# Last sums of a hybrid block: four parts in place of eight, shared by VectorE and GpSimd

## The chip, the cores and the metric

The kernel runs on one core of one Trainium2 chip. The metric is the device time in microseconds of one execution; a profiled execution also has a span, from its first to its last instruction. Engines are named as in the profile: PE is TensorE, DVE is VectorE, ACT is ScalarE, POOL is GpSimd, SP is SyncE, which here only issues DMAs. A q behind a name (SPq, ACTq) means the engine's sequencer, which issues DMAs and waits.

## The reference, cut to what matters

```python
x = x + conv_attention(group_norm(x))            # x: (32, 16, 16, 64) f32
t = to_tokens(x)                                 # 8192 tokens of 64 channels
t = t + axial_attention(layer_norm(t))
t = t + mixture_of_experts(layer_norm(t))        # 8 experts, each token goes to 2 of them
# inside: out = gate1 * expert1(token) + gate2 * expert2(token)
```

Only the last line concerns the change. For every token the result is the residual `t`, plus the gated output of its first expert, plus that of its second: two additions over 8192 x 64 numbers.

## The kernel before

The tokens lie as 128 partitions x 64 tiles x 64 channels: partition p holds tokens 64p to 64p + 63. The residual stays in SBUF the whole time (`s.x1`, called residual in the rows). The expert stage works through 39 slot tiles of tokens sorted by expert. GpSimd scatters each result row with an indirect DMA (line 1243) to `chosen_out` in HBM, which has one row of 64 floats for each token and each of its two choices. Every semaphore `added` counts the landed scatters.

After the last slot tile comes the final stage, with which the change deals:

- SP waits until all scatters have landed (`all_added`, line 1157). Then it issues eight loads of 512 KB (line 1194), two for each quarter of the tiles: the quarter of the first choices into `first`, that of the second choices into `second`. Both are halves of the buffer called norm_T in the rows. Semaphore `fin_in[q]` counts the two loads of quarter q (16 each).
- VectorE goes through eight parts of 8 tiles (`PARTS_OUT = 8`, so `EIGHTH = 8`). For each it waits for the quarter in which the part lies, adds `second` to `first` in place (line 1769), waits for that sum, and adds `first` to the residual (line 1771). The latter counts up `sum_n`.
- SP and ACT each wait for `sum_n` of a part, and each issue two stores of it (line 1160, called from two loops). A store takes 32 partitions of the part and writes rows of 256 bytes that lie 1 KB apart in the output.
- SP and ACT end when all stores have landed. GpSimd only waits in `all_added`, and does nothing else in this stage. TensorE and ACT's compute are done too.

```python
out_rows = out_dram.rearrange("b r c e -> b (r c) e").rearrange("b (g j) e -> j b g e", j=4)

def store(eng, q, j):
    eng.dma_start(out_rows[j][:, part(q), :], s.x1[j * BATCH:(j + 1) * BATCH, part(q), :]).then_inc(stored, 16)
```

The order of work on each engine is that of the code. Semaphores alone tie the engines together. SP's queue holds the eight loads and, behind them, SP's stores; ACT's queue holds only its stores.

Of the kernel before, what the change touches and what calls it, by code (L numbers as in the profile page):

```python
# [14 lines left out]
ALU = mybir.AluOpType  # L15
# [6 lines left out]
TOK = BATCH * L  # L22
# [659 lines left out]
QUARTERS = 4  # L682
# [306 lines left out]
EXPERTS, HID = 8, 682  # L989
# [5 lines left out]
REGION = TOK // SLOT  # L995
# [22 lines left out]
    return next(t for t in range(len(TABLES)) if k < sure_tiles(t) or t == len(TABLES) - 1)  # L1018

PARTS_OUT = 8

def dispatch_and_experts(nc, s, a, out_dram, sem):

    with ExitStack() as own:
# [22 lines left out]
        number, base, first_slot, tile_base = (tmp(f"rt_{n}", [P, EXPERTS]) for n in ("number", "base", "first_slot", "tile_base"))  # L1050
# [95 lines left out]
        EIGHTH = TILES // PARTS_OUT  # L1146
        first, second = (s.xt[:, i * TILES * C:(i + 1) * TILES * C].rearrange("p (t c) -> p t c", c=C) for i in range(2))
        fin_in = [sem(f"fin_loads{q}") for q in range(QUARTERS)]
        half_n, sum_n, stored = sem("fin_first_added"), sem("fin_both_added"), sem("fin_stored")
        out_rows = out_dram.rearrange("b r c e -> b (r c) e").rearrange("b (g j) e -> j b g e", j=4)  # L1150

        def part(q):
            return slice(q * EIGHTH, (q + 1) * EIGHTH)

        def all_added(eng):
            for i, landed in enumerate(added):
                eng.wait_ge(landed, adds(len(range(i, FTILES, len(added)))))
# [7 lines left out]
        with nc.Block() as block:  # L1165
            @block.sync
            def _(eng):
                eng.wait_ge(pads_n, 1)
                for i in range(2):
                    eng.dma_start(s.router[halves(i), i * EXPERTS:(i + 1) * EXPERTS], a["L1_ffn_router_w"].rearrange("e c -> c e"),  # L1170
                                  allow_slow_non_contiguous=True).then_inc(router_n, 16)
                landed = 0
                for k in range(FTILES):
                    t = table_of(k)
                    eng.wait_ge(tab_n, t + 1)
                    for m in range(landed, chunks_in_table(t)):
                        eng.wait_ge(sent[m], 16 * 2 * PAIR)
                    landed = chunks_in_table(t)
                    wait(eng, gate_n, k - 3)
                    wait(eng, ext_n, k - 3)  # L1180
                    tile = eng.value_load(table[t][0:1, k:k + 1], min_val=0, max_val=BLANK)
                    src = slot_x[bass.ds(tile, 1), 0:width(k), :]
                    for band in range(4):
                        lane = band % 2 * B32
                        eng.dma_start(x[k % 4][band * B32:(band + 1) * B32, 0:width(k)].rearrange("t (b c) -> t b c", c=B32),
                                      src[:, :, lane:lane + B32].rearrange("o (b t) c -> (o t) b c", t=B32)).then_inc(x_in[k % 4], 16)
                    eng.dma_start(gate_id[k % 4][0:depth(k), :, :], src[:, :, C:C + 2].rearrange("o (r p) c -> (o p) r c", p=depth(k)),
                                  allow_slow_non_contiguous=True).then_inc(x_in[k % 4], 16)
                eng.wait_ge(oc_n, FTILES)
                all_added(eng)  # L1190
                for q in range(QUARTERS):
                    some = slice(q * QTILES, (q + 1) * QTILES)
                    for k, into in enumerate((first, second)):
                        eng.dma_start(into[:, some, :], s.chosen_out[k * TOK:(k + 1) * TOK, :].rearrange("(p t) c -> p t c", p=P)[:, some, :]
                                      ).then_inc(fin_in[q], 16)
                for q in range(PARTS_OUT):
                    eng.wait_ge(sum_n, q + 1)
                    for j in (2, 3):
                        store(eng, q, j)
                eng.wait_ge(stored, 16 * PARTS_OUT * 4)  # L1200

            @block.gpsimd
            def _(eng):
                eng.memset(s.router[:, :], 0.0).then_inc(pads_n, 1)
                eng.memset(chosen[:, :, 0], 0.0).then_inc(const_n, 1)
                eng.memset(going_on[:, :, 0], 0.0).then_inc(const_n, 1)
                eng.memset(going_on[:, :, 1:PAIR + 1], 1.0).then_inc(const_n, 1)
                for i in range(2):
                    eng.memset(full[i][:, :], 0.0).then_inc(const_n, 1)
                    eng.memset(end[i][:, :], 0.0).then_inc(const_n, 1)  # L1210
                eng.memset(one_row[:, :], 1.0).then_inc(const_n, 1)
                eng.memset(table_f[:, :], float(BLANK)).then_inc(const_n, 1)
                eng.memset(ones[:, :], 1.0).then_inc(order_n, 1)
                for t, n, first, by in ((number, EXPERTS, EXPERTS, -1), (base, EXPERTS, 0, TOK), (first_slot, EXPERTS, 0, TOK), (tile_base, EXPERTS, 0, REGION),
                                        (step, REGION, SLOT, SLOT), (tile_no, FTILES, 0, 1)):
                    eng.iota(t[:, :], pattern=[[by, n]], base=first, channel_multiplier=0,
                             allow_small_or_imprecise_dtypes=True).then_inc(const_n, 1)
                eng.wait_ge(order_n, 1)
                eng.affine_select(out=lower[:, :], in_=ones[:, :], compare_op=ALU.is_gt, fill=0.0, base=0,
                                  pattern=[[1, P]], channel_multiplier=-1).then_inc(order_n, 1)  # L1220
                for k in range(2):
                    eng.iota(ids[:, k, :], pattern=[[1, TILES]], base=k * TOK, channel_multiplier=TILES,
                             allow_small_or_imprecise_dtypes=True).then_inc(ids_n, 1)

                def send(m, first, last, at_once):
                    if first == 0:
                        eng.wait_ge(slots_n, m + 1)
                        eng.wait_ge(rows_n, m + 1)
                        eng.wait_ge(z_n, Z * (m + 1))
                    for t in range(first, last):  # L1230
                        for k in range(2):
                            tile = m * PAIR + t
                            eng.indirect_dma_start(s.slot_x[:, :], bass.IndirectOffsetOnAxis(slot[:, k, tile:tile + 1], 0),  # L1233
                                                   rows[m % RING][:, k, t, :], None).then_inc(sent[m], 16)
                        if (t + 1 - first) % at_once == 0 or t == last - 1:
                            eng.wait_ge(sent[m], 16 * 2 * (t + 1))

                def scatter(k):
                    eng.wait_ge(oc_n, k + 1)
                    for j in range(R):  # L1240
                        if j > 0 and k + 2 < FTILES:
                            eng.wait_ge(h_n, HCHUNKS * (k + 2) + j + 1)
                        eng.indirect_dma_start(s.chosen_out[:, :], bass.IndirectOffsetOnAxis(ex_id[k % OUTS][0:depth(k), j:j + 1].bitcast(U32), 0),  # L1243
                                               out[k % OUTS][0:depth(k), j, :], None, bounds_check=2 * TOK - 1, oob_is_err=False).then_inc(added[k % OUTS], 16)

                eng.wait_ge(s.blank_n, 16)
                send(0, 0, PAIR, 1)
                send(1, 0, PAIR, 1)
                send(2, 0, 4, 1)
                send(2, 4, PAIR, 2)  # L1250
                send(3, 0, PAIR, 2)
                for k in range(FTILES):
                    m, piece = 4 + k // 3, k % 3
                    if m < PAIRS:
                        send(m, (0, 3, 6)[piece], (3, 6, PAIR)[piece], 3)
                    scatter(k)
                all_added(eng)

            @block.tensor
            def _(eng):  # L1260
# [138 lines left out]
            def _(eng):  # L1399
# [23 lines left out]
                for g in range(STEPS):  # L1423
# [9 lines left out]
                    m = chunk(g, 4)  # L1433
# [46 lines left out]
                copy_y(LAST)  # L1480
                for q in range(PARTS_OUT):
                    eng.wait_ge(sum_n, q + 1)
                    for j in (0, 1):
                        store(eng, q, j)
                eng.wait_ge(stored, 16 * PARTS_OUT * 4)
# [2 lines left out]
            def _(eng):  # L1488
# [276 lines left out]
                run(eng, body, tab_n)  # L1765
                result(LAST, LAST % OUTS)
                for q in range(PARTS_OUT):
                    eng.wait_ge(fin_in[q * QUARTERS // PARTS_OUT], 32)
                    eng.tensor_tensor(first[:, part(q), :], first[:, part(q), :], second[:, part(q), :], ALU.add).then_inc(half_n, 1)
                    eng.wait_ge(half_n, q + 1)  # L1770
                    eng.tensor_tensor(s.x1[:, part(q), :], s.x1[:, part(q), :], first[:, part(q), :], ALU.add).then_inc(sum_n, 1)  # L1771

def hybrid_block(nc, a, out):
# [59 lines left out]
```

## Time and profile before

| | us |
|---|---|
| time, median of 3 runs (lowest, highest) | 971.08 (970.32, 974.22) |
| span of the profiled execution | 969.5 |
| last scatter issued by GpSimd | 945.90 |
| first final load issued by SP | 947.96 |
| first final sum starts on VectorE | 953.26 |
| last final sum starts on VectorE | 963.32 |

The profiled execution has no device time of its own in the profile: its span is 969.5 us, 0.8 us under the fastest of the three timed runs and 1.6 us under their median. The lower four lines are starts inside that span. The final stage, from the first load to the end, is 21.5 us long, 2.2% of the span.

### The profile page before, as it was taken

How to read it: one execution, taken by the hardware profiler on the slowest of the kernel's cores; microseconds unless marked ns; L12 is line 12 of the kernel's file. 1: busy time of each engine (PE TensorE's matmuls, PEld its weight loads, DVE VectorE, ACT ScalarE, POOL GpSimd, SP SyncE). 2: the span in 40 equal slices, each digit the busy share in tenths (PEclk: the TensorE clock that was granted, in tenths of full speed). 3: DMA queues.
4: the chain of work that ended last, by engine and by line, in shares of the span. 5: the costliest groups of instructions: out<-in, count | busy, mean ns of one | idle time of the engine just before them, and what ended most of it. 6: DMA issues, size and time to landing. Idle time of an engine off the chain costs nothing.

```text
span 969.5 us, 24022 instructions
## 1 busy us (share of the span) xinstructions
PE 829.5 (86%) x8420; PEld 505.2 (52%) x8420; DVE 623.7 (64%) x1425; ACT 456.7 (47%) x894; POOL 411.0 (42%) x524
## 2 busy tenths in 40 slices
PE   4775699999999788979998877869989999999940
PEld 4544477777777665647777752223323333333430
DVE  0452487878787466753887956768756666667644
ACT  2042466666666434444554534634535555555520
POOL 0000255555545311100245555666676774444570
PEclk9975799999999879998998889989989999999985
DMA  7115300000000199000000041052133332232108
GB/s 195 55 54 123 65 9 11 8 11 8 11 8 5 54 341 328 6 2 3 11 18 19 20 65 31 24 78 44 36 57 54 57 58 46 43 48 34 20 3 260
DMA packets 156254, 56.29 MB, mean 58 GB/s; under 512 B 121103, under 2 KB 150617, under 8 KB 156176
## 3 DMA queue, kind: packets, MB, share of 16 engines
q1 hardware_dynamic: 142736, 45.69, 20.9%
q0 software_dynamic: 9088, 8.55, 2.7%
q10 hardware_dynamic: 4352, 1.05, 0.5%
q8 instruction: 45, 0.74, 0.3%
q14 instruction: 33, 0.27, 0.1%
HBM read 25.09 MB, written 28.51 MB: 55 GB/s over the span
## 4 chain that ended last, share of the span: by engine, by line
PE 35%; DVE 10%; issue 4%; POOL 3%; DMA 2%; ACT 1%; SPq 1%; ACTq 0%; DVEq 0%; POOLq 0%
PE bank L1352 17%; PE bank L1362 9%; PE bank L1292 2%; POOL chosen_out L1243 2%; PE bank L1370 2%; POOL slot_x L1233 1%; PE bank L1283 1%; DVE norm_T L1751 1%; PE bank L1265 1%; PE bank L1274 1%; PE bank L1301 1%; DVE av_og L1501 1%; DMA slot_x<-rows,slots 1%; ACT norm_T L1459 1%; DVE residual L1771 1%
## 5 line engine op out<-in xcount | busy, mean ns | idle before, releaser
L1352 PE MATMUL bank<-ex_xt,ex_w 64*114 64x512 f32 (+7 forms) x936 | 216.6, 587 | 27.0 <-DVE ex_xt L1696 13.2
L1751 DVE TENSOR_TENSOR norm_T<-norm_T,bank 114x512 f32<-114x512 f32 (+7 forms) x234 | 142.0, 630 | 100.4 <-ACT norm_T L1459 98.5
L1243 POOL DMA_INDIRECT chosen_out<-ex_out,ex_id x156 | 153.2, 982 | 118.0 <-DVE norm_T L1751 42.0
L1459 ACT ACTIVATE norm_T<-bank 114x512 f32<-114x512 f32 (+7 forms) x234 | 129.9, 558 | 93.4 <-PE bank L1352 92.2
L1233 POOL DMA_INDIRECT slot_x<-rows,slots x128 | 125.3, 979 | 111.3 <-issue 64.4
L1352 PEld LDWEIGHTS bank<-ex_xt,ex_w 64*114 64x114 f32 x936 | 76.6, 178 | 142.7 <-issue 105.2
L462 POOL TENSOR_TENSOR probs<-shifted,win_rden 128x512 f32<-128x512 f32 x64 | 66.8, 1044 | 103.3 <-DVE win_rden L656 96.7
L1362 PE MATMUL bank<-norm_T,ex_w 114*64 114x512 f32 (+7 forms) x468 | 101.9, 571 | 0.3 <-ACT ex_w L1446 0.3
L642 DVE TENSOR_REDUCE win_max<-ps_s 128x8 f32<-128x512 f32 x64 | 43.9, 686 | 35.8 <-PE ps_s L502 35.8
L1362 PEld LDWEIGHTS bank<-norm_T,ex_w 114*64 114x64 f32 x468 | 30.1, 138 | 67.9 <-issue 49.8
L1452 ACT ACTIVATE norm_T<-bank 128x512 f32<-128x512 f32 (+7 forms) x39 | 21.8, 559 | 79.9 <-PE bank L1362 79.9
L647 DVE TENSOR_TENSOR shifted<-ps_s,win_max 128x512 f32<-128x512 f32 x64 | 44.2, 691 | 4.7
L527 PE MATMUL ps_c<-xp,tap_w 128*128 128x256 f32 x288 | 45.6, 304 | 0.0
L596 ACT ACTIVATE shifted<-shifted 128x512 f32<-128x512 f32 x64 | 40.3, 631 | 10.9 <-DVE shifted L647 9.8
L652 DVE TENSOR_REDUCE win_den<-shifted 128x8 f32<-128x512 f32 x64 | 43.2, 675 | 0.1
L1292 PEld LDWEIGHTS bank<-wo_sb,av_og 128*128 128x128 f32 x256 | 31.9, 203 | 18.2 <-DVE av_og L1501 11.4
L587 ACT ACTIVATE values<-ps_yv 128x512 f32<-128x512 f32 x32 | 19.1, 598 | 44.5 <-PE ps_yv L510 44.5
L1292 PE MATMUL bank<-wo_sb,av_og 128*128 128x64 f32 x256 | 34.2, 290 | 6.5 <-DVE av_og L1501 6.5
L845 POOL TENSOR_TENSOR residual<-residual,bo_sb 128x512 f32<-128x512 f32 x8 | 10.2, 1269 | 69.6 <-DVE ax_xc L949 69.6
L938 DVE COPY ax_y<-ax_ps_y 128x512 f32<-128x512 f32 x32 | 22.1, 692 | 27.0 <-PE ax_ps_y L872 26.8
L630 DVE COPY score_side<-ps_yv 128x512 f32<-128x512 f32 x32 | 22.1, 690 | 26.3 <-PE ps_yv L489 26.3
L527 PEld LDWEIGHTS ps_c<-xp,tap_w 128*128 128x128 f32 x288 | 39.0, 191 | 0.0
(259 smaller groups left out, 1482.9 us busy)
## 6 DMA issues: line engine op xcount, KB each, us to landing
slot_x<-blank SPq DMA_DIRECT2D x1, 17028.0 KB, 56.3
ex_x<-slot_x SPq DMA_DIRECT2D x128, 64.0 KB
norm_T<-chosen_out SPq DMA_DIRECT2D x8, 512.0 KB, 7.0
w_in<-in_L_ffn_w_dram SPq DMA_DIRECT2D x24, 168.0 KB
chosen_out<-ex_out,ex_id POOLq DMA_INDIRECT x156, 2.2
wlocal_in<-in_L_conv_w_local_dram SPq DMA_DIRECT2D x2, 1152.0 KB, 7.4
norm_T<-in_x_dram SPq DMA_DIRECT2D x4, 512.0 KB, 8.8
residual<-in_x_dram SPq DMA_DIRECT2D x4, 512.0 KB, 7.6
```

The lines of the kernel that those rows point to most:

```text
L462: eng.tensor_tensor(probs[e][:, :, :], shifted[e][:, :, :], rden[e][:, :].unsqueeze(2).to_broadcast([P, HEADS, WTOK]), ALU.mult).then_inc( ...
L527: last = eng.matmul(ps_c[:, 0:L].rearrange("p (r c) -> p r c", r=SIDE), s.tap_w[:, tap].rearrange("p k c -> p (k c)"), xp[par][:, u:u + SI ...
L642: eng.tensor_reduce(mx[e][:, :], scores(e), AX.X, ALU.max).then_inc(max_n, 1)
L647: eng.tensor_tensor(shifted[e][:, :, :], scores(e), mx[e][:, :].unsqueeze(2).to_broadcast([P, HEADS, WTOK]), ALU.subtract).then_inc(sub_n, 1)
L652: eng.tensor_reduce(den[e][:, :], shifted[e][:, :, :], AX.X, ALU.add).then_inc(den_n, 1)
L1233: eng.indirect_dma_start(s.slot_x[:, :], bass.IndirectOffsetOnAxis(slot[:, k, tile:tile + 1], 0), rows[m % RING][:, k, t, :], None).then_i ...
L1243: eng.indirect_dma_start(s.chosen_out[:, :], bass.IndirectOffsetOnAxis(ex_id[k % OUTS][0:depth(k), j:j + 1].bitcast(U32), 0), out[k % OUTS ...
L1292: last = eng.matmul(ps_r[:, t * C:(t + 1) * C], og[g % 2][:, m, t * P:(t + 1) * P], s.wo[:, m, :], start=(m == 0), stop=(m == 1))
L1352: eng.matmul(ps[b][0:HCHUNK, 0:width(k)], w13[par][halves(i), c * HCHUNK:(c + 1) * HCHUNK], xt[par][halves(i), 0:width(k)], start=True, st ...
L1362: last = eng.matmul(ps_y[halves(i), 0:width(k)], w2[par][:, c, :], h[par][:, c, 0:width(k)], start=(pair == 0), stop=(pair == PAIRS_OF_CHU ...
L1459: eng.activation(act[c % DEEP][:, 0:width(k)], ps_1[c % DEEP][0:HCHUNK, 0:width(k)], ACT.Silu).then_inc(act_n, 1)
L1751: eng.tensor_tensor(h[par][:, c, 0:width(k)], act[c % DEEP][:, 0:width(k)], ps_3[c % deep3(k)][0:HCHUNK, 0:width(k)], ALU.mult).then_inc(h ...
```

## The change

`PARTS_OUT` goes from 8 to 4, so a part is a quarter of 16 tiles, and a store moves 128 KB in place of 64 KB; there are 16 stores in place of 32, with the same rows of 256 bytes. Of each part VectorE sums the first ten tiles and GpSimd the last six, each with the same two additions. GpSimd waits for `fin_in[q]` in place of `all_added`. SP and ACT wait for both engines' sums before they store a part. The renaming of loop variables on GpSimd (`first` to `start_at` and `begin`) only keeps the name `first` free for the buffer.

```diff
-PARTS_OUT = 8
+PARTS_OUT = 4
...
+        pool_half_n, pool_sum_n = sem("fin_first_added_pool"), sem("fin_both_added_pool")
...
+        def mine_and_pools(q):
+
+            cut = q * EIGHTH + 10
+            return slice(q * EIGHTH, cut), slice(cut, (q + 1) * EIGHTH)
...
                 for q in range(PARTS_OUT):
                     eng.wait_ge(sum_n, q + 1)
+                    eng.wait_ge(pool_sum_n, q + 1)
                     for j in (2, 3):
                         store(eng, q, j)
...
-                all_added(eng)
+                for q in range(PARTS_OUT):
+                    some = mine_and_pools(q)[1]
+                    eng.wait_ge(fin_in[q], 32)
+                    eng.tensor_tensor(first[:, some, :], first[:, some, :], second[:, some, :], ALU.add).then_inc(pool_half_n, 1)
+                    eng.wait_ge(pool_half_n, q + 1)
+                    eng.tensor_tensor(s.x1[:, some, :], s.x1[:, some, :], first[:, some, :], ALU.add).then_inc(pool_sum_n, 1)
...
                 for q in range(PARTS_OUT):
                     eng.wait_ge(sum_n, q + 1)
+                    eng.wait_ge(pool_sum_n, q + 1)
                     for j in (0, 1):
                         store(eng, q, j)
...
                 for q in range(PARTS_OUT):
-                    eng.wait_ge(fin_in[q * QUARTERS // PARTS_OUT], 32)
-                    eng.tensor_tensor(first[:, part(q), :], first[:, part(q), :], second[:, part(q), :], ALU.add).then_inc(half_n, 1)
+                    some = mine_and_pools(q)[0]
+                    eng.wait_ge(fin_in[q], 32)
+                    eng.tensor_tensor(first[:, some, :], first[:, some, :], second[:, some, :], ALU.add).then_inc(half_n, 1)
                     eng.wait_ge(half_n, q + 1)
-                    eng.tensor_tensor(s.x1[:, part(q), :], s.x1[:, part(q), :], first[:, part(q), :], ALU.add).then_inc(sum_n, 1)
+                    eng.tensor_tensor(s.x1[:, some, :], s.x1[:, some, :], first[:, some, :], ALU.add).then_inc(sum_n, 1)
```

GpSimd's last instructions before the change are the scatters and nothing behind them:

```order
L1243 DMA chosen_out<-ex_out,ex_id 16384x64 x112
L1165 UNCONDITIONAL_BRANCH
```

After the change eight additions stand behind the scatters:

```order
L1250 DMA chosen_out<-ex_out,ex_id 16384x64 x112
L1267 TENSOR_TENSOR norm_T<-norm_T 128x384
L1269 TENSOR_TENSOR residual<-residual,norm_T 128x384
L1267 TENSOR_TENSOR norm_T<-norm_T 128x384
L1269 TENSOR_TENSOR residual<-residual,norm_T 128x384
L1267 TENSOR_TENSOR norm_T<-norm_T 128x384
L1269 TENSOR_TENSOR residual<-residual,norm_T 128x384
L1267 TENSOR_TENSOR norm_T<-norm_T 128x384
L1269 TENSOR_TENSOR residual<-residual,norm_T 128x384
L1171 UNCONDITIONAL_BRANCH
```

So GpSimd's queue gets pairs of additions of 384 elements a partition; nothing stands behind them. On VectorE the sixteen additions of 512 elements at the program's end become eight of 640, and SP's queue has the same eight loads, then eight stores of 16 tiles where sixteen of 8 tiles stood. This is SP's end of before:

```order
L1194 DMA norm_T<-chosen_out 128x1024 x8
L1160 DMA out_dram<-residual 32x8x64 x16
```

And this is SP's end of the changed kernel:

```order
L1200 DMA norm_T<-chosen_out 128x1024 x8
L1166 DMA out_dram<-residual 32x16x64 x8
```

ACT's queue ends in the same way, with eight stores for sixteen.

## Rows read from the trace of the kernel before

**Rows 1.** Chain that ended last, window 920 to 970: start us, us, what
```profile
945.90 1.91 DMA chosen_out<-ex_out,ex_id
...
948.38 4.85 DMA norm_T<-chosen_out
...
953.26 0.70 DVE norm_T L1769
...
953.99 0.69 DVE residual L1771
954.68 0.61 DVE norm_T L1769
...
963.32 0.69 DVE residual L1771
```

**Rows 2.** Timeline, engine SP: start us, us, what
```profile
947.96 0.38 SPq L1194 DMA_DIRECT2D norm_T<-chosen_out  x1
...
951.56 0.51 SPq L1194 DMA_DIRECT2D norm_T<-chosen_out  x1
...
954.71 0.33 SPq L1160 DMA_DIRECT2D out_dram<-residual  x1
...
965.85 0.58 SPq L1160 DMA_DIRECT2D out_dram<-residual  x1
...
966.48 0.55 SPq L1160 DMA_DIRECT2D out_dram<-residual  x1
```

**Rows 3.** DMA issues, windows at 948.0, 951.7 and 966.7: KB each, us to landing
```profile
norm_T<-chosen_out SPq DMA_DIRECT2D x1, 512.0 KB, 4.0
...
norm_T<-chosen_out SPq DMA_DIRECT2D x1, 512.0 KB, 9.7
...
out_dram<-residual SPq DMA_DIRECT2D x1, 64.0 KB, 2.6
```

**Rows 4.** Windows of the final stage: columns as in its first line
```profile
core 0: us, PE busy (x) PEld busy (x) DVE busy (x) ACT busy (x) POOL busy (x), PEclk, DMA share, GB/s
947.90:948.90 1.00, 0.00 (x0) 0.00 (x0) 0.00 (x0) 0.00 (x0) 0.00 (x0) 0.50 0.00 0
...
950.00:958.00 8.00, 0.00 (x0) 0.00 (x0) 4.60 (x8) 0.00 (x0) 0.00 (x0) 0.50 0.99 387
958.00:960.50 2.50, 0.00 (x0) 0.00 (x0) 2.47 (x4) 0.00 (x0) 0.00 (x0) 0.50 1.03 365
960.50:965.00 4.50, 0.00 (x0) 0.00 (x0) 3.41 (x6) 0.00 (x0) 0.00 (x0) 0.50 1.27 282
965.00:968.50 3.50, 0.00 (x0) 0.00 (x0) 0.00 (x0) 0.00 (x0) 0.00 (x0) 0.50 1.11 230
968.50:969.50 1.00, 0.00 (x0) 0.00 (x0) 0.00 (x0) 0.00 (x0) 0.00 (x0) 0.50 0.03 5
```

**Rows 5.** DMA queues in 958 to 960.5: packets, MB, share (q1 SP, q10 ACT)
```profile
q1 hardware_dynamic: 235, 0.87, 94.4%
q10 hardware_dynamic: 188, 0.05, 8.4%
```

**Rows 6.** Groups by form, DVE: busy us, mean ns of one, idle before
```profile
L1703 DVE TENSOR_TENSOR ex_out<-ex_both_halves,ex_gate 128x256 f32<-128x256 f32 x32 | 13.6, 425 | 1.1
...
L1771 DVE TENSOR_TENSOR residual<-residual,norm_T 128x512 f32<-128x512 f32 x8 | 5.5, 692 | 0.3
```

**Rows 7.** Groups by form, POOL: busy us, mean ns of one, idle before
```profile
L462 POOL TENSOR_TENSOR probs<-shifted,win_rden 128x512 f32<-128x512 f32 x64 | 66.8, 1044 | 103.3 <-DVE win_rden L656 96.7 <-issue 6.6
...
L451 POOL TENSOR_TENSOR xp<-xw,one_of_each 128x128 fp32r<-128x128 f32 x64 | 24.3, 402 | 14.5 <-ACT xw L576 14.5
L845 POOL TENSOR_TENSOR residual<-residual,bo_sb 128x512 f32<-128x512 f32 x8 | 10.2, 1269 | 69.6 <-DVE ax_xc L949 69.6
```

**Rows 8.** Timeline around 579, 616 and 625 us, DVE and POOL
```profile
578.94 0.52 DVE L1682 TENSOR_SCALAR ex_w<-w 128x684 f32 x1
...
615.48 0.96 POOL L1233 DMA_INDIRECT slot_x<-rows,slots  x1 [0.30 <-issue]
615.99 0.76 DVE L1682 TENSOR_SCALAR ex_w<-w 128x684 f32 x1
...
625.03 0.52 DVE L1682 TENSOR_SCALAR ex_w<-w 128x684 f32 x1
625.12 1.25 POOL L1233 DMA_INDIRECT slot_x<-rows,slots  x1 [0.30 <-issue]
```

**Rows 9.** Timeline around 202 us, DVE and POOL
```profile
202.00 0.68 DVE L652 TENSOR_REDUCE win_den<-shifted 128x8 f32<-128x512 f32 x1
...
201.59 1.04 POOL L462 TENSOR_TENSOR probs<-shifted,win_rden 128x512 f32<-128x512 f32 x1 [2.68 <-DVE win_rden L656]
```

More of the change, by code:

```diff
@@ L1213, in _ @@
                 eng.memset(ones[:, :], 1.0).then_inc(order_n, 1)
-                for t, n, first, by in ((number, EXPERTS, EXPERTS, -1), (base, EXPERTS, 0, TOK), (first_slot, EXPERTS, 0, TOK), (tile_base, EXPERTS, 0, REGION),
+                for t, n, start_at, by in ((number, EXPERTS, EXPERTS, -1), (base, EXPERTS, 0, TOK), (first_slot, EXPERTS, 0, TOK), (tile_base, EXPERTS, 0, REGION),
                                         (step, REGION, SLOT, SLOT), (tile_no, FTILES, 0, 1)):
-                    eng.iota(t[:, :], pattern=[[by, n]], base=first, channel_multiplier=0,
+                    eng.iota(t[:, :], pattern=[[by, n]], base=start_at, channel_multiplier=0,
                              allow_small_or_imprecise_dtypes=True).then_inc(const_n, 1)
@@ L1223, in _, with send @@
                              allow_small_or_imprecise_dtypes=True).then_inc(ids_n, 1)
-                def send(m, first, last, at_once):
-                    if first == 0:
+                def send(m, begin, last, at_once):
+                    if begin == 0:
                         eng.wait_ge(slots_n, m + 1)
@@ L1229, in send @@
                         eng.wait_ge(z_n, Z * (m + 1))
-                    for t in range(first, last):
+                    for t in range(begin, last):
                         for k in range(2):
@@ L1234, in send @@
                                                    rows[m % RING][:, k, t, :], None).then_inc(sent[m], 16)
-                        if (t + 1 - first) % at_once == 0 or t == last - 1:
+                        if (t + 1 - begin) % at_once == 0 or t == last - 1:
                             eng.wait_ge(sent[m], 16 * 2 * (t + 1))
```

## The prediction, made before the result was known

> **What bounds the kernel now.** Everything up to the last scatter is untouched, so I read only what comes behind it. I began with the chain that ended last [rows 1]. Its end reads as if VectorE were the bound: the last scatter's DMA, then 4.85 us of loads, then sixteen additions end to end from 953.26 to 964.01, a pair every 1.33 us. That reading is incomplete, since the chain says nothing of the 5.5 us from 964.01 to the span's end, nor what the DMA engines did meanwhile.
>
> So I went to the issues and landings. The eight loads go out between 947.96 and 951.56 [rows 2]; the first lands 4.0 us after its issue and the last 9.7 us after its own [rows 3], that is at 951.96 and 961.26. Seven steps lie between: one load every 1.33 us, and a quarter (two loads) every 2.66 us. The quarters thus land at about 953.3, 955.9, 958.6 and 961.25. VectorE needs 2 x 1.33 = 2.66 us for the two parts of a quarter. It keeps pace with the loads exactly; were it faster, it would wait for them.
>
> Then the windows [rows 4]. The DMA engines are busy from 950 on without a gap, first at 387 GB/s with loads, at 282 GB/s from 960.5 to 965, when only stores are left with their rows of 256 bytes, and at 230 GB/s from 965 to 968.5. The stores issued from 954.71 on [rows 2] hardly move before 960.5: in 958 to 960.5 ACT's queue got 188 packets and 0.05 MB through beside 0.87 MB of SP's [rows 5], and in SP's queue the stores stand behind the loads. All 2.10 MB of stores but 0.05 MB go out between 960.5 and 968.5. The bound of the stage is therefore the DMA engines' work, loads and then stores, and not the sums. The sums have to be early enough, no more.
>
> **The change part by part.** The chain is cut into three terms: when the last part's sums are done, when its stores have gone out, and what is left behind the last packet.
>
> *Loads.* The same eight, issued at the same time behind the same wait of SP. No edit touches them: 0. GpSimd's `all_added` goes; SP's own stays and gates the loads, so this is worth 0 too.
>
> *VectorE.* It loses sixteen additions of 512 elements and gets eight of 640. One of 256 elements with both inputs in SBUF takes 425 ns and one of 512 takes 692 [rows 6], so 1.04 ns an element, and 640 cost 0.692 + 128 x 0.00104 = 0.83 us. A part is 1.65 us of VectorE.
>
> *GpSimd.* It gets eight additions of 384 elements, which the trace does not have. Between 128 elements (402 ns) and 512 (1044 ns) the slope is 1.67 ns and the fixed part 188 ns, and 384 would cost 0.83 us; but those operations have a second input that is one number repeated. Line 845, which adds into the residual with whole rows on both sides, takes 1269 ns for 512, so 2.11 ns an element over the same fixed part and 1.00 us for 384 [rows 7]. It is the same addition on the same tile; I take 1.00, with 0.83 as the lower bound. A part is 2.00 us of GpSimd.
>
> *The two beside each other.* This decides the sign. If they don't disturb each other, a part takes 2.0 us plus a semaphore or two, under the 2.66 us of the loads, and the last sums are done at 961.25 + 2.1 = 963.35, against 964.01 before. If they take turns, a part costs 1.65 + 2.00 = 3.65 us, more than its loads, the four run back to back from 953.26, and the last sums are done at 953.26 + 4 x 3.65 = 967.9. No row has such a pair of additions side by side. The nearest are those of [rows 8]. VectorE's copy of 684 weights takes 0.52 us alone, 0.76 us when it begins 0.51 us into a GpSimd operation that has 0.45 us left. GpSimd's takes 0.96 us there, and 1.25 us when it begins 0.09 us into VectorE's copy. So whoever comes second stands still for part of the other's time: these two engines do hold each other up in SBUF. Against it: GpSimd's multiplication of 512 took its 1.04 us, and VectorE's reduction beginning inside it its 0.68 us [rows 9]; but that VectorE operation reads one tensor, where the final additions read two. I take turns as the likelier, at the full 3.65 us; at least 2 x (0.83 + 0.83) = 3.3 us if GpSimd is as fast as its lower bound.
>
> The Trainium skill, SBUF — State Buffer, section "Who interferes with whom", says that a VectorE instruction with two SBUF inputs contends with a GpSimd instruction that reads SBUF, since its second input comes through a read interface that the two share, and that the one that comes first holds it for the whole instruction. By that rule the pace is the 3.65 us of the turns. No run here shows it for two additions; [rows 8, 9] are in line with it.
>
> *Stores.* Sixteen issues for thirty-two, the same bytes in the same 256-byte packets. With turns, parts 0 to 2 are summed at 956.9, 960.6 and 964.2. The first two wait behind the loads anyhow, and go out by about 960.5 + 1.0/0.282 = 964.1; part 2 follows, out by about 967. The last part is then alone: 0.03 us to the issue, 0.95 us from issue to first packets (as from the load issued at 947.96, with nothing moved up to 948.90 [rows 2, 4]), 0.524 MB at 282 GB/s = 1.86 us, and 1.0 us from the last packets at 968.5 to the end at 969.5 [rows 4]: 3.84 us in all. 967.9 + 3.84 = 971.7, against 969.5: **+2.2 us**.
>
> *The waits.* SP and ACT wait for the later of two semaphores; behind that wait stand only stores, for which nobody but the end waits. One sum that is late holds back all 128 KB stores of its part: that is in the 3.84 us.
>
> The sum is against the span of 969.5 us. The median of the timed runs is 1.6 us above it, which I leave as it is: 971.1 + 2.2 = **973.3 us**.
>
> **The rivals.**
>
> *No interference.* With the last sums done at 963.35 the stores are never short of work: 2.05 MB at 282 GB/s from 960.5 are out at 967.8, plus 1.0 is 968.8, so -0.7 us and 970.4. The gain comes from the stretch at 230 GB/s at the end of before, in which SP's queue issued a 64 KB store every 0.6 us [rows 2] and had little in hand; half the issues, with all parts ready sooner, would keep the engines at 282. That the sums run on two engines gains nothing by itself. For it: [rows 9]. Against it: [rows 8]. Chance 0.28. It becomes a loss only if a part takes longer than (969.5 - 3.84 - 953.26) / 4 = 3.1 us, so half interference would still be no loss.
>
> *Turns at the lower bound.* 3.3 us a part: last sums at 966.5, end at 970.4, +0.9 us, 972.0. Chance 0.17.
>
> *Store bound by its descriptors.* If the 230 GB/s of 965 to 968.5 is the rate at which queues fill and larger stores keep to it throughout, 2.05 MB take 8.9 us: end at 970.4, +0.9 us and 972.0, with or without turns. Against it: 282 GB/s for 4.5 us before. Chance 0.06.
>
> *Slower by more than can be told from noise.* Each hand-over between the engines costs time of its own. Two a pair of additions, 16 in all. At 0.3 us each, the whole by which GpSimd's operation grew in [rows 8], that is 4.8 us more: end at 976.5, +7.0 us, 978.1. It takes 0.17 us a hand-over for the total to pass 4.9 us. Against it: in [rows 8] each was held up by less than the time the other had left (0.24 of 0.45, 0.29 of 0.43), so a hand-over costs nothing there. Chance 0.04.
>
> **How the numbers follow.** My forecast, turns at full length, has 0.45. What two measurements of this kernel can tell apart is about 0.5%, 4.9 us; only the hand-over case, and a gain nobody can find in a stage whose DMA engines are never idle, lie outside. So same 0.95, slower 0.03, faster 0.02. The range is no interference below (970.4) and full turns above (973.3), each with about 1 us for the spread of the three runs, a little more above, where the hand-over case and the 974.22 of one run lie: 969.4 to 975.2.
>
> **What would show it.** In the changed profile: VectorE's additions of 640 at 0.83 us alone, or some at 1.5 to 1.8 us with turns; GpSimd's of 384 at 1.00 us alone, or up to 1.8; a part every 3.65 us in place of 2.66; DMA engines idle or slack between about 967 and 969; the last sums at 967.9. If instead the last sums are done near 963.4 and stores flow at 282 GB/s to the end, the step on turns is wrong. If the loads land at other times than a quarter every 2.66 us from 953.3, or GpSimd's first addition starts late after its scatters, the frame is wrong.

## The result

| | before | changed |
|---|---|---|
| median of 20 runs, us (lowest, highest) | 971.47 (967.07, 977.73) | 977.49 (974.09, 986.11) |
| span of the profiled execution, us | 969.5 | 976.1 |

The changed kernel is slower: the ratio is 1.0066 with a 95% interval of 1.0047 to 1.0086, or 6.0 us between the medians. The prediction had 973.3 us and a range to 975.2, and gave 0.95 to "no difference that can be told". It missed the time and the range, and by its own line of 4.9 us, which 6.0 us passes, also the likeliest case.

The profiled execution of the changed kernel issues its first final load at 948.84 us, 0.9 us later than before, though nothing ahead of it was touched. In the ten runs below that add nothing ahead of it, that moment lies anywhere between 945 and 953 us. So I measure the final stage by itself, from the issue of its first load to the end of the span: 969.5 - 947.96 = 21.5 us before, 976.1 - 948.84 = 27.2 us after. The stage explains 5.7 us.

These rows of the changed kernel's timeline (start us, us, what) answer to [rows 1, 6, 7]:

```profile
948.84 4.17 SPq L1200 DMA_DIRECT2D norm_T<-chosen_out  x8
954.20 0.83 DVE L1783 TENSOR_TENSOR norm_T<-norm_T 128x640 f32<-128x640 f32 x1 [17.25 <-DMA norm_T<-chosen_out]
954.25 1.62 POOL L1267 TENSOR_TENSOR norm_T<-norm_T 128x384 f32<-128x384 f32 x1 [6.63 <-DMA norm_T<-chosen_out]
955.06 1.50 DVE L1785 TENSOR_TENSOR residual<-residual,norm_T 128x640 f32<-128x640 f32 x1
955.95 1.46 POOL L1269 TENSOR_TENSOR residual<-residual,norm_T 128x384 f32<-128x384 f32 x1
956.75 1.34 DVE L1783 TENSOR_TENSOR norm_T<-norm_T 128x640 f32<-128x640 f32 x1 [0.19 <-DMA norm_T<-chosen_out]
957.37 1.57 POOL L1267 TENSOR_TENSOR norm_T<-norm_T 128x384 f32<-128x384 f32 x1
...
958.12 1.50 DVE L1785 TENSOR_TENSOR residual<-residual,norm_T 128x640 f32<-128x640 f32 x1
959.02 1.46 POOL L1269 TENSOR_TENSOR residual<-residual,norm_T 128x384 f32<-128x384 f32 x1
...
962.08 1.46 POOL L1269 TENSOR_TENSOR residual<-residual,norm_T 128x384 f32<-128x384 f32 x1
...
965.15 1.46 POOL L1269 TENSOR_TENSOR residual<-residual,norm_T 128x384 f32<-128x384 f32 x1
```

The first addition of VectorE takes the 0.83 us forecast for it alone, although GpSimd's begins 0.05 us behind it; that one takes 1.62 us. All later ones of VectorE take 1.34 to 1.61 us, and GpSimd's 1.46 to 1.57. From one of GpSimd's second sums to the next (962.08 to 965.15) a part takes 3.07 us. The turns are there. But the last sum is done at 966.6, 17.8 us into the stage, against 16.1 before. That is 1.7 us, not 5.7.

The windows (columns as in [rows 4]) show where the rest lies:

```profile
961.00:965.00 4.00, 0.00 (x0) 0.00 (x0) 3.93 (x4) 0.00 (x0) 3.92 (x3) 0.50 1.24 281
965.00:970.30 5.30, 0.00 (x0) 0.00 (x0) 0.76 (x1) 0.00 (x0) 1.53 (x2) 0.50 0.95 189
...
967.00:968.00 1.00, 0.00 (x0) 0.00 (x0) 0.00 (x0) 0.00 (x0) 0.00 (x0) 0.50 0.48 89
968.00:969.00 1.00, 0.00 (x0) 0.00 (x0) 0.00 (x0) 0.00 (x0) 0.00 (x0) 0.50 1.14 225
969.00:970.00 1.00, 0.00 (x0) 0.00 (x0) 0.00 (x0) 0.00 (x0) 0.00 (x0) 0.50 1.03 200
...
970.30:976.00 5.70, 0.00 (x0) 0.00 (x0) 0.00 (x0) 0.00 (x0) 0.00 (x0) 0.50 0.00 0
```

The slack of the DMA engines that the prediction expected between 967 and 969 is there, from 967 to 968. But in the last 5.7 us no engine computes and the DMA engines move nothing. Before, this dead end was 1.0 us long. To see what runs there I asked for the instructions of the line that closes the block, where all engines meet. These are sequencer rows. The page has none of them in its groups, and the changed kernel's chain has only the first 1.49 us of the long one. They give engine, operation, ns, first and last start in us.

```profile
L1171 POOLq DRAIN  x1: 10732/10732/10732, 965.1 to 965.1; - x1
L1171 SPq COMPARE_BRANCH  x1: 41/41/41, 970.8 to 970.8; - x1
```

```profile
L1165 POOLq DRAIN  x1: 9212/9212/9212, 948.2 to 948.2; - x1
L1165 SPq COMPARE_BRANCH  x1: 41/41/41, 969.1 to 969.1; - x1
```

There it was just as long, but began at 948.2, when GpSimd had nothing left to do, and was over at 957.4, 11.7 us ahead of the stores.

### The profile page after: what moved, and what is told of

Read it like the earlier page. It is cut to its first block, busy times and chain, and to the rows that moved or that the text cites. A ratio compares the mean times of both kernels' runs of the same rounds, so it can differ in the third digit from the quotient of the medians.

```text
span 976.1 us, 24009 instructions
## 1 busy us (share of the span) xinstructions
PE 831.6 (85%) x8420; PEld 503.6 (52%) x8420; DVE 623.5 (64%) x1417; ACT 456.4 (47%) x894; POOL 421.7 (43%) x532
## 3 DMA queue, kind: packets, MB, share of 16 engines
q1 hardware_dynamic: 142608, 45.69, 21.1%
## 4 chain that ended last, share of the span: by engine, by line
PE 29%; POOL 7%; DMA 7%; issue 5%; DVE 3%; ACT 1%; SPq 1%; POOLq 0%; ACTq 0%; DVEq 0%
PE bank L1364 17%; PE bank L1374 9%; DMA slot_x<-rows,slots 6%; POOL slot_x L1240 4%; POOL chosen_out L1250 2%; PE bank L1382 2%; DVE norm_T L1764 1%; DMA ex_gate_id<-slot_x 1%; POOL norm_T L1267 1%; ACT norm_T L1471 1%; PE bank L1304 1%; PE bank L1277 1%; SPq L1191 1%; DMA norm_T<-chosen_out 1%; POOL residual L1269 0%
## 5 line engine op out<-in xcount | busy, mean ns | idle before, releaser
L1364 PE MATMUL bank<-ex_xt,ex_w 64*114 64x512 f32 (+7 forms) x936 | 220.1, 596 | 25.1 <-DVE ex_xt L1709 10.9
L489 PE MATMUL ps_yv<-xw,score_w 64*128 64x256 f32 x256 | 37.2, 410 | 1.9 <-DVE values L635 1.4
```

Source lines behind the costliest of these rows:

```text
L1364: eng.matmul(ps[b][0:HCHUNK, 0:width(k)], w13[par][halves(i), c * HCHUNK:(c + 1) * HCHUNK], xt[par][halves(i), 0:width(k)], start=True, st ...
```

## The experiments

Theory A says that GpSimd's closing DRAIN is the loss: it costs 9.2 us behind GpSimd's last instruction, and the changed kernel moved that instruction from 948 to 966.6. Theory B is what the prediction rested on: the turns, the late sums, the stores behind them. Each run has its stage (first load's issue to end of span) from its own profile. Single stages differ by some tenths of a us without a cause in the code: e3 and e10 have the same sums and stores, and differ by 0.4 us.

| run | edit | stage, us | ratio to before (95%) |
|---|---|---|---|
| before | | 21.5 | |
| changed | | 27.2 | 1.0066 (1.0047 to 1.0086) |
| e1 | before, GpSimd waits for the last sum | 26.0 | 1.0035 (1.0016 to 1.0054) |
| e2 | changed, no DRAIN of GpSimd | 22.5 | 0.9993 (0.9971 to 1.0014) |
| e3 | four parts, sums on VectorE alone | 21.2 | 0.9986 (0.9967 to 1.0005) |
| e4 | e1 with a DRAIN ahead of the wait | 21.5 | 1.0000 (0.9980 to 1.0020) |
| e5 | before, no DRAIN of GpSimd | 21.6 | 0.9995 (0.9974 to 1.0017) |
| e7 | changed, VectorE waits for GpSimd in each part | 25.9 | one execution |
| e8 | changed, GpSimd in parts 0 and 1 alone | 21.4 | 1.0009 (0.9987 to 1.0031) |
| e9 | changed, VectorE reduces in place of adding | 24.9 | one execution |
| e10 | e3, no DRAIN of GpSimd | 21.7 | 1.0004 (0.9979 to 1.0029) |
| e11 | DRAIN, then GpSimd in parts 2 and 3 | 21.4 | 1.0006 (0.9982 to 1.0030) |

### e1: the DRAIN moved, nothing else

```diff
                     scatter(k)
                 all_added(eng)
+                eng.wait_ge(sum_n, PARTS_OUT)
```

> The kernel before with one edit: GpSimd, behind its last wait, also waits until VectorE's eighth and last final sum is done. It computes nothing more. Theory A (GpSimd's closing DRAIN): the DRAIN of 9.2 us, which ran hidden from 948.17 to 957.39 us, now begins near 964.0 and ends near 973.3, and the program ends with it: span about +3.9 us against before, last store landing unchanged near 969.1. Theory B (the 6.6 us come from the turns of VectorE and GpSimd and the later stores alone): nothing takes turns here, so the span is unchanged, within 0.5 us.

The stage is 26.0 us, +4.5. GpSimd does no work that the kernel before didn't do, and no transfer is later: SP's last wait passes 21.1 us into the stage, as before. Its closing line:

```profile
L1165 POOLq DRAIN  x1: 9212/9212/9212, 966.4 to 966.4; - x1
L1165 SPq COMPARE_BRANCH  x1: 41/41/41, 970.9 to 970.9; - x1
```

The DRAIN runs from 966.4 to 975.6 and the span ends at 975.8. The stage grows by 0.6 us more than expected: here the last sum came 0.2 us later in the stage than before, and the DRAIN began 0.3 us behind it. Theory B falls for the larger part of the loss.

### e2: the changed kernel without the DRAIN

```diff
-        with nc.Block() as block:
+        with nc.Block(no_gpsimd_drain=True) as block:
```

> The changed kernel, whose last block is closed without GpSimd's DRAIN; all of GpSimd's DMAs have been waited for by semaphore before. Theory A: the 5.1 us between the last store's landing and the end go, the end is about 0.3 us behind the landing near 970.7: span about 971.1, +1.6 us against before and -5.0 against the changed kernel. Theory B: no change against the changed kernel, +6.6 us.

```profile
L1171 SPq COMPARE_BRANCH  x1: 41/41/41, 968.4 to 968.4; - x1
```

SP passes its wait for the stores at 968.4, and the span ends at 968.9. The stage is 22.5 us, 4.7 less than the changed kernel's, with the same turns. What is left of the loss is 1.0 us, and that is theory B's share. From the last sum (964.26) to the end it takes 4.6 us. Timing can't tell this kernel from the one before.

### e3: four parts alone

```diff
-PARTS_OUT = 8
+PARTS_OUT = 4
```

> The kernel before with four parts in place of eight, all sums on VectorE; GpSimd as before. Both theories: VectorE needs 2 x 1.36 us for 16 tiles, as long as a quarter takes to load, so the last sums are done near 964.0 as before, and 128 KB stores change the rest: between -0.7 us (stores at 282 GB/s to the end) and +1.0 us (the last part is twice as large behind the last sum). It separates the store size from the sharing.

The stage is 21.2 us, 0.3 less than before; the ratio's interval includes 1. An addition of 1024 elements takes 1226 ns. From the start of the first to the end of the last, a quarter's sums take 2.49 us, where the four of before took 2.75, and the last sum of all is done 0.5 us earlier in the stage. The larger stores cost nothing that can be seen.

### e4: a DRAIN ahead of the wait

```diff
                 all_added(eng)
+                eng.drain()
+                eng.wait_ge(sum_n, PARTS_OUT)
```

> As e1, with an explicit DRAIN on GpSimd in front of the added wait. Theory A1 (a DRAIN clears away what the indirect DMAs left, once): the explicit one takes 9.2 us from about 948 and is hidden, the closing one behind the last sum is short (under 0.1 us), and the span is that of before. Theory A2 (every DRAIN of GpSimd behind indirect DMAs takes 9.2 us, however often): the closing one takes 9.2 us again, and the span is +3.9 us as in e1. Theory B: unchanged span.

A1 holds. The added DRAIN and the closing one:

```profile
L1258 POOLq DRAIN  x1: 9210/9210/9210, 950.0 to 950.0; - x1
...
L1165 POOLq DRAIN  x1: 38/38/38, 966.2 to 966.2; - x1
```

The first takes the 9.2 us, hidden, and the second 38 ns. So the DRAIN has something to clear only once (that it clears is inferred from its lengths), and the loss of e1 is gone though GpSimd ends as late.

### e5: the DRAIN taken from the kernel before

The edit is that of e2, on the kernel before.

> The kernel before, its last block closed without GpSimd's DRAIN. The DRAIN of before ends at 957.4, 11.7 us ahead of the last store's landing. Theory A: it is wholly hidden there, so its absence changes nothing (within 0.3 us of span, apart from the run's own variation ahead of the last stage). If it also disturbed the loads that run beside it (theory C: the e2 gain is not only from the end), the stage from first load to end would be over 0.5 us shorter than 21.55 us.

The stage is 21.6 us, the same. Where the DRAIN is covered it costs nothing, and it doesn't disturb the loads beside it.

### e6 and e12: what makes the DRAIN long

In e6 DRAINs stand ahead of the first indirect DMA, behind sends 0 and 1 (16 indirect DMAs each), behind the scatters of slot tiles 6, 14 and 26, and twice at the end. In e12 one stands behind slot tile 34, and one at the end with 16 indirect DMAs between them.

```diff
                 eng.wait_ge(s.blank_n, 16)
+                eng.drain()
                 send(0, 0, PAIR, 1)
+                eng.drain()
                 send(1, 0, PAIR, 1)
+                eng.drain()
...
                     scatter(k)
+                    if k in (6, 14, 26):
+                        eng.drain()
                 all_added(eng)
+                eng.drain()
+                eng.drain()
```

> The kernel before with DRAINs of GpSimd added: before the first indirect DMA, behind 16 and 32 of them, behind the scatters of slot tiles 6, 14 and 26, and two directly one behind the other at the end. Theory A1 (a DRAIN clears what has gathered since the last one): the first takes under 0.1 us, the middle ones grow with the number of indirect DMAs since the one before, the last one is short. Theory A3 (a fixed cost for any DRAIN that follows indirect DMAs): each middle one takes about 9.2 us whatever the number, and only the second of the two at the end is short. The drains delay the kernel; its time is not the question.

> The kernel before with one added DRAIN of GpSimd behind the scatters of slot tile 34, so that only 16 indirect DMAs lie between it and one more at the end, which is then as undisturbed as the closing one of before. Measured at the same place so far: 9.21 us with 284 indirect DMAs and no DRAIN since the start of the stage, 3.96 us with 48 since the last DRAIN. If the length grows with their number on a straight line through these two, the one at the end takes 3.2 us; if it is in proportion to their number, 1.3 us or less; if it depends on something else of the run (a fixed cost with two levels), 3.96 us again.

```profile
L1247 POOLq DRAIN  x1: 1109/1109/1109, 438.0 to 438.0; - x1
...
L1249 POOLq DRAIN  x1: 1376/1376/1376, 506.2 to 506.2; - x1
...
L1251 POOLq DRAIN  x1: 1359/1359/1359, 540.3 to 540.3; - x1
...
L1261 POOLq DRAIN  x3: 5177/11586/17737, 697.6 to 881.3; - x3
...
L1263 POOLq DRAIN  x1: 3964/3964/3964, 965.0 to 965.0; - x1
...
L1264 POOLq DRAIN  x1: 46/46/46, 969.0 to 969.0; - x1
```

And in e12, the last DRAIN but one:

```profile
L1260 POOLq DRAIN  x1: 1361/1361/1361, 954.9 to 954.9; - x1
```

Behind 16 indirect DMAs it takes 1.36 us, three times alike (1376, 1359, 1361 ns); behind 48, with all engines at rest, 3.96 us; behind none, 0.05 us at the end. That is 83 to 86 ns an indirect DMA, all of whose data had landed already. So the length is no fixed cost (A3 falls), and the straight line that I expected in e12 (3.2 us) falls too.

The other DRAINs can't be read by their length. A DRAIN can begin while GpSimd still has instructions to run. The longest of e6 began at 781.0; its row, and GpSimd's rows behind it:

```profile
L1261 POOLq DRAIN  x1: 17737/17737/17737, 781.0 to 781.0; - x1
```

```profile
792.93 0.98 POOL L1243 DMA_INDIRECT chosen_out<-ex_out,ex_id  x1 [0.30 <-issue]
799.50 0.98 POOL L1243 DMA_INDIRECT chosen_out<-ex_out,ex_id  x1 [5.58 <-issue]
```

It was over at 798.70, only 4.79 us behind GpSimd's last instruction (793.91). The first DRAIN of e6, at 438.0, ran in the same way beside constants that GpSimd was writing, and was over 0.07 us behind them. Here is what each took from the end of GpSimd's last instruction, or from its own start where that was later:

| DRAIN | indirect DMAs since the one before | us |
|---|---|---|
| e6, behind sends 0 and 1; e12, at the end | 16 | 1.38, 1.36, 1.36 |
| e6, behind slot tile 26, and at the end | 48 | 3.97, 3.96 |
| e6, behind slot tile 14 | 58 | 4.79 |
| e6, behind slot tile 6 | 98 | 8.06 |
| e12, behind slot tile 34 | 268 | 7.92 |
| before, e1, e3, e4, e11 | 284 | 9.21 |

Up to 98 the numbers lie on one line, 0.05 us and 0.082 us an indirect DMA, also in the midst of the experts, where VectorE was busy and the last scatters had not landed when GpSimd was through. The two long counts lie on the same line if 172 fewer are counted in both: 96 and 112. So this is no upper limit, since 16 more still cost 1.29 us; something had cleared 172 of them without a DRAIN. It wasn't GpSimd's waits for its sends, nor the place in the program: in e6 the sends count, each waited for, and the 58 span the last sends. What it was stays open.

### e7: how long the additions are alone

```diff
                     some = mine_and_pools(q)[0]
                     eng.wait_ge(fin_in[q], 32)
+                    eng.wait_ge(pool_sum_n, q + 1)
```

> The changed kernel, with VectorE waiting for GpSimd's two sums of a part before it begins its own two, so that GpSimd's first part runs alone. If the engines exclude each other wholly when side by side, GpSimd's 384 take 0.71 us alone ((3.07 - 2 x 0.83) / 2) and VectorE's 0.83; if they exclude each other only in part, GpSimd's take about 1.00 us alone, and the pace of 3.07 us was less than the 3.66 us of all four. GpSimd goes on to the next part while VectorE sums, so later ones overlap. Theory A for the end: GpSimd ends earlier than VectorE, and the closing DRAIN ends 9.24 us behind GpSimd's last sum or not at all later than the stores.

```profile
953.60 0.99 POOL L1267 TENSOR_TENSOR norm_T<-norm_T 128x384 f32<-128x384 f32 x1 [6.74 <-DMA norm_T<-chosen_out]
954.66 0.99 POOL L1269 TENSOR_TENSOR residual<-residual,norm_T 128x384 f32<-128x384 f32 x1
...
965.12 0.81 DVE L1784 TENSOR_TENSOR norm_T<-norm_T 128x640 f32<-128x640 f32 x1
965.96 0.83 DVE L1786 TENSOR_TENSOR residual<-residual,norm_T 128x640 f32<-128x640 f32 x1
```

Alone, GpSimd's 384 take 0.99 us and VectorE's 640 0.81 to 0.83 us. The four of a part add up to 3.6 us, and side by side they took 3.07. The rows of the changed kernel show where the difference lies. Its additions end in turn: one of VectorE 0.68 us behind the one of GpSimd before it (959.62 and 958.94), one of GpSimd 0.86 us behind the one of VectorE (960.48 and 959.62). Each is 0.13 to 0.15 us short of its length alone. So they exclude each other but for that much of each instruction, 0.5 to 0.6 us a part; that it is the start of an instruction is my reading. The end is theory A's again: GpSimd's last sum is done at 964.5 and its DRAIN at 973.75, 2 us behind the stores.

### e8: GpSimd's help in the first two parts alone

```diff
-            cut = q * EIGHTH + 10
+            cut = q * EIGHTH + (10 if q < 2 else EIGHTH)
```

GpSimd's loop and the waits for its sums end with part 1.

> The changed kernel, but GpSimd helps only with parts 0 and 1; VectorE sums all 16 tiles of parts 2 and 3. Theory A: GpSimd's last sum ends 6.1 us earlier, 11.6 us behind the first load's issue, the DRAIN ends at about 20.9 us behind it, just hidden behind the stores (21.1 in the kernel before), and the stage is 21.3 to 22.0 us long: same as before, 5.5 us less than the changed kernel. If the DRAIN is not the cause but GpSimd's work as such, half the loss stays: +2.9 us.

```profile
L1171 POOLq DRAIN  x1: 10731/10731/10731, 956.8 to 956.8; - x1
...
L1171 SPq COMPARE_BRANCH  x1: 41/41/41, 967.8 to 967.8; - x1
```

The DRAIN is over at 967.5, 0.3 us ahead of the stores, and the stage is 21.4 us. Half the help with the same turns costs nothing, not half the loss.

### e9: VectorE with one input

```diff
-                    eng.tensor_tensor(first[:, some, :], first[:, some, :], second[:, some, :], ALU.add).then_inc(half_n, 1)
+                    eng.tensor_reduce(both[:, 0, 0:10], second[:, some, :], AX.X, ALU.add).then_inc(half_n, 1)
...
-                    eng.tensor_tensor(s.x1[:, some, :], s.x1[:, some, :], first[:, some, :], ALU.add).then_inc(sum_n, 1)
+                    eng.tensor_reduce(both[:, 1, 0:10], first[:, some, :], AX.X, ALU.add).then_inc(sum_n, 1)
```

> The changed kernel in which VectorE does not add: in place of each addition of 640 it reduces 640 elements of one SBUF tensor into ten numbers, so the residual of its ten tiles stays without the experts' results. Theory D (only VectorE's second input from SBUF collides with GpSimd's reads): VectorE's 640 take about 0.82 us each and GpSimd's 384 about 0.99 us each beside them, a part's sums are done 2.1 us behind its loads and the last at about 15.2 us behind the first load's issue. Theory E (any SBUF operand collides): a part still takes about 3.07 us. Either way the DRAIN ends the program 9.2 us behind GpSimd's last sum.

```profile
950.61 0.82 DVE L1783 TENSOR_REDUCE ex_both_halves<-norm_T 128x10 f32<-128x640 f32 x1 [17.41 <-DMA norm_T<-chosen_out]
950.66 0.99 POOL L1267 TENSOR_TENSOR norm_T<-norm_T 128x384 f32<-128x384 f32 x1 [6.78 <-DMA norm_T<-chosen_out]
951.46 0.82 DVE L1785 TENSOR_REDUCE ex_both_halves<-norm_T 128x10 f32<-128x640 f32 x1
951.73 0.99 POOL L1269 TENSOR_TENSOR residual<-residual,norm_T 128x384 f32<-128x384 f32 x1
```

Side by side, both run at their lengths alone, so theory E falls. Theory D fits, but it is not shown that the second input alone makes the difference: the reduction also writes ten numbers in place of 640, and in [rows 8] VectorE's copy of 684, with one input, and GpSimd's indirect DMAs held each other up. Of what the Trainium skill says in SBUF — State Buffer, "Who interferes with whom", this case agrees on which instructions collide (e9 against the changed kernel). The section calls this contention an exclusive lock; that the first holds it for its whole instruction it spells out for VectorE's two-port mode only. For the additions here that is a little too strong (3.07 us a part, not 3.6).

This run also parts the DRAIN from the turns. There are none, and GpSimd's last sum is done at 960.5, 15.4 us into the stage, earlier than the last sum of before. Yet the end is again the DRAIN's:

```profile
L1171 POOLq DRAIN  x1: 10269/10269/10269, 959.5 to 959.5; - x1
...
L1171 SPq COMPARE_BRANCH  x1: 41/41/41, 966.3 to 966.3; - x1
```

It is over at 969.74, 3.4 us behind the stores, and the stage is 24.9 us.

### e10 and e11: versions without the loss

e10 is e3 with the edit of e2. e11 has a DRAIN between GpSimd's scatters and its sums, and lets it help only with parts 2 and 3:

```diff
-            cut = q * EIGHTH + 10
+            cut = q * EIGHTH + (10 if q >= 2 else EIGHTH)
...
-                for q in range(PARTS_OUT):
+                all_added(eng)
+                eng.drain()
+                for q in range(2, PARTS_OUT):
```

SP's and ACT's waits, and GpSimd's own, are counted to match.

> Four parts, all sums on VectorE, and no DRAIN of GpSimd at the end. From the runs so far: the stage is 21.25 us long as with four parts alone, and the hidden DRAIN's absence gives 0 on top: -0.3 us against before, which timing can't tell from none (ratio 0.9985 to 1.0015).

> The changed kernel, with an explicit DRAIN of GpSimd between its scatters and its sums, and GpSimd helping only with parts 2 and 3, whose loads land when that DRAIN is over. Theory A1: the explicit DRAIN takes 9.2 us and is hidden, the closing one 0.04 us, and the stage is 21.0 to 21.8 us long, as before, although GpSimd's last sum ends as late as in no other version without a loss (some 16 us behind the first load's issue). If GpSimd's late work as such costs the time, the span stays over 4 us longer.

```profile
L1265 POOLq DRAIN  x1: 9210/9210/9210, 947.6 to 947.6; - x1
...
L1171 POOLq DRAIN  x1: 1556/1556/1556, 963.0 to 963.0; - x1
```

In e11 GpSimd's last sum is done at 964.5, 16.9 us into the stage and 0.8 us later than the last sum of before. The closing DRAIN began under that addition and is over 0.07 us behind it. The stage is 21.4 us. In e10 it is 21.7 us, 0.4 longer than in e3: the last quarter's loads landed late, and VectorE waited 0.47 us for them. No version beats the kernel before by anything that timing can tell. The best stage is e3's, 0.3 us shorter, which is within what e3 and e10 differ by.

## Why the prediction was wrong

- **The step that failed** is "what is left behind the last packet", 1.0 us, read from 968.5 to 969.5 before. I took the last store's landing for what ends the program. But the end is where all engines meet, and the meeting also waits for GpSimd's DRAIN, 9.2 us behind GpSimd's last instruction. The section on the change says that nothing stands behind GpSimd's sums; the DRAIN does. It cost 4.7 us (changed kernel against e2), 4.5 us with nothing else changed (e1). From the measured last sum, 17.8 us into the stage, 9.2 us of DRAIN and 0.2 us behind it give the 27.2 us of stage. From the forecast last sum (967.9) they would have given 979.0 us, 1.5 too much, for the turns were set too long.
- **GpSimd's `all_added`, costed at 0:** right about the wait, and beside the point. Until the change GpSimd was through at 948 and had 11.7 us of cover left. No step named what GpSimd's idle end hid.
- **Turns of VectorE and GpSimd:** the mechanism was right, the size was not. Their lengths alone were as worked out from rows (0.83 and 1.00 predicted, 0.83 and 0.99 measured), but a part took 3.07 us, not 3.65, since 0.13 to 0.15 us of each instruction overlap. The last sum came 1.7 us later than before in the stage, not 3.9. The cost of it in the end is 1.0 us (e2), where the forecast had 2.2.
- **"The last part is then alone", 3.84 us,** was too short, where the turns were too long. At 3.07 us a part the prediction's sum gives 953.26 + 12.28 + 3.84 = 969.4 us, no loss at all. But without the DRAIN it still took 4.6 us from the last sum to the end (e2). The stores of the last part went out at 225 and 200 GB/s (968 to 970 in the changed kernel), not at 282.
- **DMA engines as the bound of the stage,** until the DRAIN takes over: not contradicted. In e3 the last sum is done 0.5 us earlier and the stage is only 0.3 us shorter; in e11 it is done 0.8 us later, and the stage is no longer.
- **Larger stores:** right that they cost nothing that can be seen (e3, e10).
- **The rivals:** "hand-overs cost time of their own" gave 978.1 us, near the 977.49 measured, but that is chance: hand-overs cost less than nothing (3.07 against 3.6 us). "No interference" is refuted by the additions of 1.5 us.
- **The chance of 0.95 for no difference** rested on a list of mechanisms that all lay in sums and stores. The unlisted one was larger than all of them.

## What to carry to other kernels

Before work is given to an engine that idles at the end, ask what its idle time hides: for GpSimd behind indirect DMAs that is the closing DRAIN, which neither the page's groups nor the chain of before show, but the rows of the block's closing line do. Read what ends the program from the last sequencer row of every engine, and give each engine its slack; here GpSimd could have worked until about 959.9 us (the stores' 969.1 less 9.2), and what goes past that is paid in full: e8 stayed 0.3 us inside it and lost nothing. Read a DRAIN by its end, less the end of the last instruction ahead of it on its engine; its start says little. If it has to work later, a DRAIN in an idle gap behind its last indirect DMA takes the cost there (e4, e11).

## What the runs showed of the hardware

- Behind GpSimd's last instruction its DRAIN took 1.36 us behind 16 indirect DMAs, 3.96 us behind 48, 4.79 behind 58 and 8.06 behind 98 (e6, e12), about 0.082 us each; 0.04 to 0.07 us when another DRAIN had gone before. Behind 268 and 284 it took 7.92 and 9.21 us, as for 96 and 112.
- An addition with both inputs in SBUF on VectorE and one on GpSimd mostly took 1.5 and 1.46 to 1.62 us side by side, against 0.83 and 0.99 alone; beside a reduction of one input to ten numbers on VectorE, 0.82 and 0.99.
- One VectorE addition of 1024 elements took 1226 ns, one of 512 692 ns.
